# Order of the key blocks in the causal attention stage of a transformer block: diagonal blocks moved ahead of the plain ones

## Chip, cores and metric

The kernel runs on one core of a Trainium2 chip. The metric is the device time of one execution in microseconds (us). Before the change the median of three runs is 844.02 us (841.11 to 846.14).

## The reference

Input x is (2, 1024, 256), fp32. The block is an adaLN transformer layer:

```
h = layernorm(x) * (1 + ca) + sa
q, k, v = h@wq, h@wk, h@wv          # 32 query heads, 8 key/value heads, head size 8
att = softmax(causal(q k^T / sqrt(8)))
x = x + ga * ((att v) @ wo)
h = layernorm(x) * (1 + cb) + sb
x = x + gb * (shared MLP(h)/5 + top-4-of-16 experts(h) * 4/5)
```

The change touches only the causal softmax attention: for every query row the exponentials of the scores against all keys at or before it, and their products with v. A sum over key blocks may be taken in any order.

## The kernel before

**The attention stage.** Work is done in 16 groups (2 batches x 8 key/value heads, 4 query heads each). The queries of a group, 1024 rows, are two halves of 512; the keys are eight blocks of 128, c = 0 to 7. `half_steps` (L58) lists the steps of a half as (half, blocks, slots). Half 0 has three steps: block 0, then block 2, then blocks 1 and 3 side by side. Half 1 has seven: blocks 0, 1, 2, 3, 4, then block 6, then 5 and 7. Ten steps, numbered 0 to 9, make `STEPS`. A diagonal block (0, 1, 2, 3 of half 0, and 4, 5, 6, 7 of half 1) needs a causal mask; blocks 0 to 3 of half 1 are plain. Block c covers only the queries from its diagonal on, so block 6 (and 2) has 256 columns for each head and fits in one score slot instead of two.

**One step on TensorE (L1322 to L1339).** In this order: score slot 0 (`scores`, L1246), one `wide` product (L1182), score slot 1, one `narrow` product (L1194), then the product of the probabilities of the step two back with v (`product(s - 2)`, L1265), then the third slot if the step has one. Score slots take turns on two pairs of PSUM banks: slot k may be written once ScalarE is done with slot k - 2 (`released`, L1197). `wide` and `narrow` belong to a pass one and a half groups ahead that finds the row maxima; VectorE reduces them (L1434 to L1454), ten pairs per group. Pair number 5 + s of the next group runs in step s below 5, pair s - 5 of the group after it in the steps from 5 on.

**ScalarE (L1007 to L1044)** takes the slots in the same order: an exponential of 128x1024 (L1034), for the one-slot blocks L1029, and in the slots listed in `DIFF_AT` a Relu of 128x1024 (L960, `exceeding`). Such a slot holds a product of the queries with differences of keys (`differences`, L1221) for a later group: entry (s, slot): (which, ahead). Difference 0 and 1 are for the group two ahead, 2 for the next. The Relu result (`over`, `over6`) goes into the narrow reductions of tiles 6 and 7. Difference 0 waits for the late keys of that group (`ky_in`, loaded by SyncE, L666). The sums of the previous group are copied in step 1 (L1000), w_hi is filled in step 8 of groups 0 to 3 (L1044), and a square root with its table loads stands in step 3 of group 14.

**GpSimd (L852 to L898)**, in order by step: the mask of each diagonal step (`affine_select`, L862, waits for that step's exponentials); w_lo in step 4 of groups 1 to 4 (L869); in step 5 `split_rows` (L833, L835), which prepares the row maxima of the next group once VectorE has turned them; in step 6 one piece of other work: in groups 2 to 9 a 1.5 MB fill of a DRAM buffer with zeros (L879), later some small products. In step 8 of the last group one scatter (L540).

**SyncE (L719 to L741)**, in order for a group: when all score slots of the group before are full, the stacks and the late keys for the group two ahead (L475, L477, L488), the sums out (L708), then `rows_in`: four writes of the split row maxima to DRAM (L697, waits for `split_rows`), a wait for their landing, two loads of them into the query stack (L702), then the score keys for the group two ahead (L488). The next group's step 0 waits for those two loads (`row_in`, L1233).

After the attention stage come the output product, routing, the shared MLP and the expert tiles, behind a barrier of all engines.

```
L58  def half_steps(half):
L93  DIFF_AT = {(1, 1): (2, 1), (6, 2): (0, 2), (8, 1): (1, 2)}
L94  SLOT_ORDER = [(s, k) for s in range(NSTEP) for k in range(3 if (s, 2) in DIFF_AT else 2)]
L418 DIAG = [s for s, (half, blocks, _) in enumerate(STEPS) if blocks[0] >= half * (TC // 2)]
```

Of the kernel before, what the change touches and what calls it, by code (L numbers as in the profile page):

```python
# [56 lines left out]

def half_steps(half):  # L58
    d = half * (TC // 2)
    return [(half, (c,), 2) for c in range(d + 1)] + [(half, (d + 2,), 1), (half, (d + 1, d + 3), 2)]  # L60


STEPS = half_steps(0) + half_steps(1)
NSTEP = len(STEPS)
SCORE_SLOTS = sum(n for _, _, n in STEPS)
# [24 lines left out]


DIFFS = 3
DIFF_AT = {(1, 1): (2, 1), (6, 2): (0, 2), (8, 1): (1, 2)}  # L93
SLOT_ORDER = [(s, k) for s in range(NSTEP) for k in range(3 if (s, 2) in DIFF_AT else 2)]  # L94

DIFF_FREE = (0, 8 - NPAIR, 4)
# [23 lines left out]
def block_kernel(nc, x_in, wq_in, wk_in, wv_in, wo_in, wr_in, we1_in, we3_in, we2_in,  # L120
# [11 lines left out]
    with whole:  # L132
# [478 lines left out]
        def slots(group, s):  # L611

            return SCORE_SLOTS * group + sum(n for _, _, n in STEPS[:s + 1])

        def banks_of(group, s, slot):
            first = 2 * ((len(SLOT_ORDER) * group + SLOT_ORDER.index((s, slot))) % 2)
            return slice(first, first + 2)
# [7 lines left out]
        with nc.Block() as block:  # L625
# [277 lines left out]
            def _(act):  # L903
# [98 lines left out]
                def early_sums():  # L1002
                    act.wait_ge(pv_done, NSTEP * (GROUPS - 1) + len(half_steps(0)))
                    act.wait_ge(y_out, 16 * (GROUPS - 1))
                    act.activation(y_sb[:, 0, :], bank[sum_bank][:, :], ACT.Copy).then_inc(y_done, 1)

                for group in range(GROUPS):  # L1007
                    for s, (half, blocks, n) in enumerate(STEPS):
# [9 lines left out]
                        to = probs[(NSTEP * group + s) % (LAG + 1)]  # L1018
                        for slot in range(3 if (s, 2) in DIFF_AT else 2):
                            banks = banks_of(group, s, slot)  # L1020
                            if (s, slot) in DIFF_AT:
                                which, ahead = DIFF_AT[s, slot]
                                if group + ahead < GROUPS:
# [24 lines left out]
            def _(pe):  # L1048
# [148 lines left out]
                def released(group, s, slot):  # L1197
# [5 lines left out]
                    if group < 0:  # L1203
                        if before == -2:
                            pe.wait_ge(over_done, DIFFS + 2)
                    elif (s, slot) not in DIFF_AT:
                        pe.wait_ge(p_full, slots(group, s) - STEPS[s][2] + 1 + slot)
                    elif group + DIFF_AT[s, slot][1] < GROUPS:
                        which, ahead = DIFF_AT[s, slot]
# [42 lines left out]
                def product(group, s):  # L1252

                    half, blocks, n = STEPS[s]
                    if s == 0 and group:
                        pe.wait_ge(y_done, group)
                    elif group == GROUPS - 1 and s == len(half_steps(0)):
                        pe.wait_ge(y_done, GROUPS)
                    pe.wait_ge(p_full, slots(group, s))
                    if s in DIAG:  # L1260
                        pe.wait_ge(p_masked, NDIAG * group + DIAG.index(s) + 1)
                    for c, off, col, width in pieces(half, blocks):
                        at = HD + 1 + (group * TC + c) * VB - half * (HD + 1)
                        for h in range(REP):
                            last = pe.matmul(bank[sum_bank][32 * h:32 * h + 32, off:TT], v_aug[:, at:at + 32],  # L1265
                                             probs[(NSTEP * group + s) % (LAG + 1)][:, h, col:col + width], start=(s == 0),
                                             stop=(s == NSTEP - 1), skip_group_check=True)
                    last.then_inc(pv_done, 1)
# [711 lines left out]
```

## Time and profile before

| | |
|---|---|
| median of three runs | 844.02 us |
| the profiled execution | 843.63 us |
| its span | 841.4 us |
| TensorE busy | 722.4 us (86%) |
| VectorE busy | 540.6 us (64%) |
| ScalarE busy | 494.4 us (59%) |
| GpSimd busy | 269.8 us (32%) |
| mean granted TensorE clock | 0.92 |

The profile is of one execution. Its own time is 843.63 us, 2.2 us more than its span. PE is TensorE's matmuls and PEld its weight loads, DVE is VectorE, ACT ScalarE, POOL GpSimd, SP SyncE. The attention groups run from about 83 us to 480 us of the span. In a row of the timeline the columns are start, length, engine, line, operation, out<-in, shape, count, and in brackets how long the engine had been idle and what released it.

### The profile page before, as it was taken

Reading aid. Unit: us, or ns where it says so; the run is one execution under the profiler, and the core shown is the slowest. Engines: PE = TensorE matmul, PEld = TensorE weight load, DVE = VectorE, ACT = ScalarE, POOL = GpSimd, SP = SyncE. Lnnn points to the kernel's source line nnn. Section 1 sums busy time; section 2 is a strip of 40 time slices with the busy share of each in tenths; the row PEclk is TensorE's granted clock in tenths of the full one; section 3 lists DMA queues with packets and bytes.
Section 4 is the critical chain, followed back from the end, with each engine's and each line's share of the span. In section 5 each row is a group of like instructions: output and inputs, shape, how many; then the busy total and the mean of one; then the engine's idle time right before and its main releaser. Section 6 shows DMA issues by size and latency. Waiting matters only on the chain. (4 is left out here: it accounts for less than half of the span.)

```text
span 841.4 us, 14770 instructions
## 1 busy us (share of the span) xinstructions
PE 722.4 (86%) x4980; PEld 455.9 (54%) x4980; DVE 540.6 (64%) x1159; ACT 494.4 (59%) x739; POOL 269.8 (32%) x332
## 2 busy tenths in 40 slices
PE   8999999999999999999989881898149967999495
PEld 7466444444444444444435460786138846788384
DVE  7667888888888888888676431657025524665177
ACT  4332599998888898889566610574016624663132
POOL 6520133323222223323111466003730061412641
PEclk9989699999999999999988986899559978999898
DMA  6846234555545543354000287034325554653322
GB/s 208 209 123 169 82 90 102 145 165 152 146 144 154 158 146 104 92 137 136 17 14 17 70 278 242 7 114 157 125 97 162 163 163 132 205 178 116 98 69 81
DMA packets 78580, 108.71 MB, mean 129 GB/s; under 512 B 16200, under 2 KB 60040, under 8 KB 77420
## 3 DMA queue, kind: packets, MB, share of 16 engines
q1 hardware_dynamic: 67996, 77.16, 32.1%
q0 software_dynamic: 9280, 29.11, 10.5%
q10 hardware_dynamic: 1232, 1.51, 0.6%
q8 instruction: 42, 0.69, 0.4%
q14 instruction: 30, 0.25, 0.1%
HBM read 59.92 MB, written 47.39 MB: 128 GB/s over the span
## 5 line engine op out<-in xcount | busy, mean ns | idle before, releaser
L1034 ACT ACTIVATE probs<-psum 128x1024 f32<-128x1024 f32 x256 | 246.9, 1027 | 49.7 <-PE psum L1246 49.2
L1434 DVE TENSOR_REDUCE max_parts<-psum 128x2 f32<-128x1024 f32 (+2 forms) x160 | 196.0, 1225 | 68.8 <-PE psum L1182 66.9
L1265 PE MATMUL psum<-probs,v_aug 128*32 128x512 f32 (+3 forms) x1536 | 162.6, 512 | 0.3 <-POOL probs L862 0.2
L862 POOL TENSOR_SCALAR_AFFINE_SELECT probs<-probs 128x512 f32<-128x512 f32 (+1 forms) x96 | 79.2, 826 | 225.9 <-ACT probs L1034 206.3
L1246 PE MATMUL psum<-qs,ks 64*128 64x512 f32 (+3 forms) x768 | 138.3, 400 | 11.3 <-ACT over L960 5.0
L1246 PEld LDWEIGHTS psum<-qs,ks 64*128 64x128 f32 x768 | 67.2, 190 | 110.5 <-ACT probs L1034 69.4
L1769 PE MATMUL psum<-w_all,v_aug 128*128 x376 | 102.2, 396 | 0.9 <-issue 0.8
L1678 ACT ACTIVATE v_aug<-psum 128x128 f32<-128x128 f32 x94 | 26.1, 277 | 103.8 <-PE psum L1769 59.6
L1670 ACT ACTIVATE v_aug<-psum,modc 128x128 f32<-128x128 f32 x188 | 75.7, 454 | 12.5 <-remote 8.8
L1182 PE MATMUL psum<-km,qs 64*128 64x128 f32 (+2 forms) x608 | 76.3, 325 | 5.8 <-DVE max_parts L1434 2.7
L1769 PEld LDWEIGHTS psum<-w_all,v_aug 128*128 128x128 f32 x376 | 74.1, 199 | 13.1 <-issue 2.3
L1861 DVE TENSOR_TENSOR v_aug<-v_aug,psum 128x128 f32<-128x128 f32 x94 | 26.9, 287 | 76.2 <-ACT v_aug L1678 66.0
L1631 POOL DMA_INDIRECT h_t<-y_sorted,posi x32 | 31.0, 969 | 128.2 <-DMA y_sorted<-late 88.2
L1265 PEld LDWEIGHTS psum<-probs,v_aug 128*32 128x32 f32 x1536 | 34.4, 111 | 67.7 <-issue 62.9
L1194 PE MATMUL psum<-km,qs 64*128 64x512 f32 x160 | 66.5, 416 | 0.4 <-DVE max_parts L1453 0.2
L1780 PE MATMUL psum<-ident,v_aug 128*128 128x128 f32 x94 | 27.1, 288 | 46.3 <-issue 26.1
L1182 PEld LDWEIGHTS psum<-km,qs 64*128 64x128 f32 x608 | 52.0, 191 | 17.5 <-DVE max_parts L1434 9.8
L1786 PE MATMUL psum<-w_all,v_aug 128*128 x188 | 60.9, 408 | 0.0
L960 ACT ACTIVATE over<-psum 128x1024 f32<-128x1024 f32 x48 | 49.3, 1026 | 10.9 <-DVE max_parts L1453 5.1
L540 POOL DMA_INDIRECT x_sorted<-probs,posi x32 | 30.7, 960 | 66.3 <-DVE posi L309 56.9
L1874 DVE TENSOR_TENSOR late<-psum,gate 128x256 f32<-128x256 f32 x94 | 39.5, 420 | 19.2 <-remote 9.0
L1648 ACT ACTIVATE km<-wmod_sb 128x512 fp32r<-128x512 f32 x16 | 10.1, 631 | 62.5 <-remote 35.0
(194 smaller groups left out, 1076.2 us busy)
## 6 DMA issues: line engine op xcount, KB each, us to landing
late<-x_sorted SPq DMA_DIRECT2D x94, 128.0 KB
y_sorted<-late SPq DMA_DIRECT2D x94, 128.0 KB
x_sorted<-g_rows POOLq DMA_DIRECT2D x6, 1536.0 KB, 7.4
qs<-q_parts SPq DMA_DIRECT2D x62, 128.0 KB
km<-k_parts SPq DMA_DIRECT2D x62, 96.0 KB
km<-k_parts SPq DMA_DIRECT2D x64, 64.0 KB
ks<-k_parts SPq DMA_DIRECT2D x64, 64.0 KB
y_sums<-g_sign SPq DMA_DIRECT2D x16, 256.0 KB, 2.8
```

Source lines behind the costliest of these rows:

```text
L862: pool.affine_select(out=tile, in_=tile, compare_op=ALU.is_ge, fill=0.0, base=0, pattern=[[0, REP], [0, n], [1, P]], channel_multiplier=-1 ...
L960: act.activation(to, psum[:, banks, :], ACT.Relu).then_inc(over_done, 1)
L1034: act.activation(to[:, 2 * slot:2 * slot + 2, off:TT], psum[:, banks, off:TT], ACT.Exp, scale=SCALE).then_inc(p_full, 1)
L1182: last = pe.matmul(bank[wide_bank + hp][:, k * w:(k + 1) * w], qs[buf][rows, hh, i * P:(i + 1) * P], km[buf][rows, at:at + w], start=(k == ...
L1194: pe.matmul(bank[narrow_bank][:], qs[buf][rows, hh, i * P:(i + 1) * P], km[buf][rows, KU:KU + TT], start=True, stop=True).then_inc(narrow_ ...
L1246: last = pe.matmul(bank[first + hp][:, to:to + width], ks[buf][rows, c * P:(c + 1) * P], qs[buf][rows, hh, half * TT + off:(half + 1) * TT ...
L1265: last = pe.matmul(bank[sum_bank][32 * h:32 * h + 32, off:TT], v_aug[:, at:at + 32], probs[(NSTEP * group + s) % (LAG + 1)][:, h, col:col ...
L1434: dve.tensor_reduce(out=max_parts[:, :, h0:h1, slice(*tiles), slot], in_=psum[:, wide_bank:wide_bank + 2, :].rearrange("p a (s w) -> p (a ...
L1670: last = act.activation(xt[:, k % 2, c * P:(c + 1) * P], bank[X_BANKS[k % 2]][:, c * P:(c + 1) * P], ACT.Identity, scale=modc[:, b, 1, c, ...
L1769: last = pe.matmul(bank[U_BANKS[k % 2]][:, 0:2 * H], xt[:, k % 2, c * P:(c + 1) * P], w_all[:, bass.ds(expert[k], 1), c * 2 * H:(c + 1) * ...
L1786: pe.matmul(bank[Y_BANKS[k % 2]][:, 0:D], gt[:, k % 2, :], w_all[:, bass.ds(expert[k], 1), W13:WCOLS].rearrange("p a n -> p (a n)"), start ...
L1874: dve.tensor_tensor(out=yt[:, k % NY, :], in0=bank[Y_BANKS[k % 2]][:, 0:D], in1=gate[:, 1, k // TILES, :], op=ALU.mult).then_inc(y_copied, 1)
```

## The change

In half 1 the steps are now block 0, then block 4, then block 6, then blocks 5 and 7, then the plain blocks 1, 2, 3. So steps 4, 5, 6 are the diagonal ones and 7, 8, 9 the plain ones; before, steps 4, 5, 6 were plain (blocks 1, 2, 3) and 7, 8, 9 diagonal (4, 6, 5 and 7). Half 0 stays. Difference 0 moves from the third slot of step 6 to the free second slot of step 5, difference 1 from the second slot of step 8 to a third slot of step 7. Everything that is bound to a step's number (maxima pairs, split_rows, w_lo, the fill, w_hi) keeps its number. `DIAG` follows from the list.

```
 def half_steps(half):
     d = half * (TC // 2)
-    return [(half, (c,), 2) for c in range(d + 1)] + [(half, (d + 2,), 1), (half, (d + 1, d + 3), 2)]
+    return [(half, (0,), 2)] + [(half, (d,), 2)] * (half > 0) + [(half, (d + 2,), 1), (half, (d + 1, d + 3), 2)] + \
+        [(half, (c,), 2) for c in range(1, d)]
...
-DIFF_AT = {(1, 1): (2, 1), (6, 2): (0, 2), (8, 1): (1, 2)}
+DIFF_AT = {(1, 1): (2, 1), (5, 1): (0, 2), (7, 2): (1, 2)}
```

## Rows read from the trace of the kernel before

**Rows 1.** Busy time by stretch: one stretch of steady groups, one of group 13

```profile
180.00:240.00 60.00, 58.92 (x534) 27.94 (x530) 50.35 (x82) 54.30 (x59) 18.59 (x24) 1.00 0.51 141
...
426.00:429.00 3.00, 2.54 (x13) 1.04 (x17) 2.96 (x14) 1.86 (x2) 0.96 (x2) 0.61 0.00 0
```

**Rows 2.** Timeline, TensorE, from step 2 of one group to step 2 of the next

```profile
301.99 0.51 PE L1246 MATMUL psum<-qs,ks 64*128 64x384 f32 x4
...
304.44 0.50 PE L1246 MATMUL psum<-qs,ks 64*128 64x512 f32 x2
...
306.14 0.49 PE L1246 MATMUL psum<-qs,ks 64*128 64x512 f32 x2
...
307.03 0.51 PE L1246 MATMUL psum<-qs,ks 64*128 64x512 f32 x2
...
308.69 0.50 PE L1246 MATMUL psum<-qs,ks 64*128 64x512 f32 x2
...
311.02 0.50 PE L1246 MATMUL psum<-qs,ks 64*128 64x512 f32 x2
...
312.15 1.06 PE L1265 MATMUL psum<-probs,v_aug 128*32 128x512 f32 x8
...
313.61 0.50 PE L1246 MATMUL psum<-qs,ks 64*128 64x512 f32 x2
...
314.76 0.50 PE L1246 MATMUL psum<-qs,ks 64*128 64x512 f32 x2 [0.42 <-ACT over L960]
...
316.42 0.50 PE L1246 MATMUL psum<-qs,ks 64*128 64x256 f32 x4
...
320.77 0.50 PE L1246 MATMUL psum<-qs,ks 64*128 64x512 f32 x2
...
322.46 0.50 PE L1246 MATMUL psum<-qs,ks 64*128 64x256 f32 x4
...
323.37 0.49 PE L1221 MATMUL psum<-km,qs 64*128 64x512 f32 x2
...
325.02 0.51 PE L1246 MATMUL psum<-qs,ks 64*128 64x384 f32 x4
```

**Rows 3.** Timeline, ScalarE, same group

```profile
305.04 3.77 ACT L1034 ACTIVATE probs<-psum 128x1024 f32<-128x1024 f32 x4 [0.48 <-PE psum L1246]
...
313.68 1.03 ACT L960 ACTIVATE over<-psum 128x1024 f32<-128x1024 f32 x1
...
314.60 1.93 ACT L1034 ACTIVATE probs<-psum 128x1024 f32<-128x1024 f32 x2
```

**Rows 4.** Line L1044, all its instructions (ns min/median/max)

```profile
L1044 ACT ACTIVATE w_hi<-wmod_sb x4: 846/846/847, 111.4 to 180.6; 128x768 fp32r<-128x768 f32 x4
```

**Rows 5.** Timeline, TensorE, the last product of the attention stage

```profile
478.61 1.07 PE L1265 MATMUL psum<-probs,v_aug 128*32 128x384 f32 x16 [0.23 <-POOL probs L862]
```

**Rows 6.** Timeline, GpSimd and SyncE, same group as rows 2

```profile
302.24 4.11 SPq L488 DMA_DIRECT2D km<-k_parts  x6
...
309.60 0.21 POOL L833 CAST neg_parts<-neg_max_t 128x32 fp32r<-128x32 f32 x1 [3.88 <-DVE neg_max_t L1465]
...
310.18 1.73 SPq L697 DMA_DIRECT2D max_rows<-neg_parts  x4
...
316.89 0.55 SPq L702 DMA_DIRECT2D qs<-max_rows  x2
```

**Rows 7.** Line L862, all its instructions of one group (ns min/median/max)

```profile
L862 POOL TENSOR_SCALAR_AFFINE_SELECT probs<-probs x6: 677/678/1099, 298.1 to 318.1; 128x512 f32<-128x512 f32 x4, 128x1024 f32<-128x1024 f32 x2
```

**Rows 8.** Timeline, SyncE, group 10, which has no fill

```profile
333.57 1.75 SPq L697 DMA_DIRECT2D max_rows<-neg_parts  x4
337.05 0.53 SPq L702 DMA_DIRECT2D qs<-max_rows  x2
```

**Rows 9.** DMA issues: KB each, median us from issue to landing

```profile
x_sorted<-g_rows POOLq DMA_DIRECT2D x6, 1536.0 KB, 7.4
...
wmod_sb<-in_L_ffn_ws_dram SPq DMA_DIRECT2D x12, 128.0 KB, 2.6
```

## The prediction

> **What bounds it now.** I read the busy time by stretch first: in 60 us of steady groups TensorE is busy 58.92 us and ScalarE 54.30 [rows 1]. Two engines are nearly full, so the order in which they hand slots to each other can matter. Then the timeline of one group, step by step [rows 2]. A group takes 325.02 - 301.99 = 23.03 us. The first score products of steps 2 to 1 start at 301.99, 304.44, 306.14, 308.69, 311.02, 313.61, 316.42, (step 9 has no row) 320.77, 322.46.
>
> An undisturbed step is step 6 without its third slot: 1.13 us from its first score product to its v product (311.02 to 312.15), then 0.99 us to the next work; 2.12 us. The third slot adds 0.47 (313.61 - 311.02 - 2.12). A v product of a one-slot block is shorter: step 3, whose product is that of block 2, takes 1.70, so 0.42 less. Steps 2 and 5 take 2.45 and 2.33 for reasons that stay with their number or with half 0 (a maxima product in many pieces, about 0.2; blocks side by side, about 0.1). Three steps are longer than this: step 4, 2.55 for 2.12; step 7, 2.81 for 2.12; step 1, 2.56 for 2.12. The excess is 0.43, 0.69 and 0.44, together **1.56 us of stall** a group, and each lies ahead of the second slot: that starts 0.89, 1.15 and 0.91 us after the first (307.03, 314.76, 323.37), 0.46 without a stall.
>
> Who is late is seen on ScalarE [rows 3]. Back to back, ScalarE takes 0.94 to 0.97 us a slot, and TensorE may write slot k about 1.05 us after ScalarE began slot k - 2: the Relu begins at 313.68, the slot it frees starts at 314.76. ScalarE begins about 0.60 us after the score products start (304.44, 305.04). So where TensorE's steps are short (3 and 0, 1.70 us, against 1.94 for two slots) or ScalarE has three slots (step 6, and step 1 with the copy of the sums), the next second slot comes late. One slot of buffering takes up the rest.
>
> **The change, part by part.**
>
> *Order of the steps.* The light v product (block 6) leaves step 0 and goes to step 7, two after its block. Step 0 becomes 2.12 us for ScalarE's 1.94, so ScalarE no longer enters step 1 late: the 0.44 of step 1 goes. Step 3 is still 1.70, so the 0.43 of step 4 stays.
>
> *Third slot.* It moves from step 6 to 7, where it meets that light product: TensorE needs 2.12 - 0.42 + 0.47 = 2.17 us, ScalarE three slots, 2.9. Followed with the numbers above, from the first score product of step 7 at 0: exponentials begin at 0.60 and 1.57, the Relu at 2.54, step 8's first slot may start at 1.57 + 1.05 = 2.62 (0.45 late), its second at 2.54 + 1.05 = 3.59 at the earliest, where 2.62 + 0.47 = 3.09 would be free: 0.50 late. So 0.95 in place of step 7's 0.69. Step 0 gets about 0.03. Sum of stalls after: 0.43 + 0.95 + 0.03 = 1.41 for 1.56: **0.15 us less a group**, 13 steady groups (0 to 12), -1.9 us. The same recurrence put on the order before gives 0.45, 0.65 and 0.45, so it is good to 0.1 a group, 1.3 us in all.
>
> *w_hi* [rows 4], 0.85 us of ScalarE, groups 0 to 3. It followed step 8 when ScalarE had a gap; now it follows the run of slots that bounds step 8. Bounds: nothing, or 0.85 x 4 = 3.4 us. Step 9 has 0.15 to 0.2 of slack a step and the stall of step 0 is gone, so I take 0.2 a group, +0.8.
>
> *Groups 13 and 14*, where output products and transposes make TensorE wait for VectorE; the work of TensorE is the same. The clock is already down to 0.61 in a stretch of group 13 [rows 1]. A light product moved beside waits: between -0.5 and +0.5, zero taken. Slots without a difference product make small bubbles in groups 14 and 15; before there were as many.
>
> *Masks.* The last v product of the stage waited 0.23 for GpSimd [rows 5]; now it needs no mask, but the product ahead of it is full, 0.42 more: +0.2. Otherwise the masks of steps 4 to 6 (0.68 us, 1.10 for blocks side by side) [rows 7] have over a step before the v product wants them, and no TensorE row of the group waits for GpSimd. The scatter that stood ahead of the last masks loses its place there; the scatters start sooner, but what follows waits for the barrier.
>
> *GpSimd's queue.* `split_rows` now stands behind the masks of steps 4 and 5. It began at 309.60 [rows 6], 0.91 after step 5 (308.69). The exponential of step 5's one slot ends at 0.60 + 1.03 = 1.63 after it (a slot of the same size in [rows 3]), the mask takes 0.68, so it begins at 2.3: 1.4 us later. The fill is issued behind the mask of step 6: its second exponential ends 1.57 + 1.03 = 2.6 us after step 6's start, the mask takes 1.1; step 6 starts 2.33 after step 5, so the fill leaves at 6.1 after step 5, where it was right behind `split_rows`. SyncE's chain: the four writes of the maxima start at 2.9 (before 1.49). With the fill beside them, SyncE had to wait from 311.91 to 316.89 for their landing; without it (group 10) from 335.32 to 337.05, 1.7 us [rows 6, 8]. Now they are out before the fill: 2.9 + 1.75 + 1.7 = 6.4 after step 5, where it was 8.2. SyncE comes to its loads sooner. The next step 0 comes 12.1 after step 5, so the loads have 5.7 us; they now run beside the fill. I take that as hidden, cost 0.
>
> *Difference 0* is wanted at step 5's second slot, near 309.4, and no longer behind step 6's v product (312.15 + 0.99 = 313.14). Its keys are the last four of the loads issued up to 302.24 + 4.11 = 306.35 [rows 6]; a load of 128 KB lands 2.6 us after issue [rows 9], and the last one is issued at 305.7, so by 308.3. Margin 1.1 us, cost 0.
>
> Sum: -1.9 + 0.8 + 0 + 0.2 = -0.9 us on the profiled 843.63, that is 842.7. The median of the runs is 0.4 above that execution: **843.1**. A measurement of this kernel tells about 0.5% (4.2 us) from no change, so this is no difference.
>
> **Rivals.**
>
> *A, faster.* The stall of step 1 goes and the one of step 8 does not grow. For it: the recurrence takes ScalarE's 0.97 a slot, and runs of four go at 0.94; 0.44 x 13 = 5.7 less. Against it: three slots in a row cannot be had under 2.8 us. Time 843.6 - 5.7 = 837.9, say 838.
>
> *B, slower: the row maxima meet the fill.* Place: the two loads L702, waited for at the next step 0. They leave at 6.4 after step 5 and the fill at 6.1. The writes in the same position before waited until 316.89, while the fill, issued right behind `split_rows` (309.60 and half a microsecond) and 7.4 us from issue to landing [rows 6, 9], ended near 317.5. If the loads too land only with the fill, that is 6.1 + 7.4 = 13.5 after step 5, where step 0 wants them at 12.1: 1.4 us in each of 8 groups, 11 us, 855. It decides from 5.7 us of landing on; the writes needed 5.0 to 6.7. Against it: the fill's data starts later than its issue, and the loads have a head start.
> The Trainium skill (DMA: Bandwidth & Descriptors, Queues, rings and completion order) says that each DMA engine takes turns between its queues a packet at a time. By that rule, the loads share rather than wait, and the trace agrees so far: the writes [rows 6] were stretched and not stopped.
>
> *C, slower: late keys.* If their landing takes 4.2 us from issue, difference 0 waits 0.5 us in 12 groups, 6 us: 849. Against it: the 2.6 us of a larger load.
>
> *D, slower: the clock.* Step 8 now has two stalls in a row, 0.95. In group 13, after waits of 0.4 to 0.75, the clock fell to 0.61 for 3 us [rows 1]. One such fall a group, 1.5 us each, 13 groups: 20 us, 863. Against it: 0.69 in one step left it at 1.00.
>
> **Numbers.** Forecast 0.68, A 0.12, B 0.11, C 0.05, D 0.04. Of the forecast's case 0.03 lies under -4.2 us. Faster 0.15, same 0.65, slower 0.20. The range reaches down to A and up to C with w_hi's upper bound (3.4 in place of 0.8), 838 to 852, which leaves out B's price, D and a little of A, under 0.2.
>
> **What would show it.** Right: group period 22.8 to 23.0; step 1 without a stall; step 8 near 3.1 us; step 7 at 2.17; writes L697 about 1.4 us later after step 5, and the wait ahead of L702 under 2 us in all groups. Wrong: a wait for `qs<-max_rows` or `km<-k_parts` ahead of step 0 or step 5, a clock under 1.00 before group 13, step 0 longer than 2.5 in groups 1 to 4, or a period off by more than 0.3.

## Result and profile after

The changed kernel takes 850.32 us, median of 19 runs, beside 844.58 us for the kernel before, also in 19 runs: ratio 1.0059, 95% interval [1.0031, 1.0087]. The medians are of all runs; the ratio, here and below, leaves out runs in a slower state, more than 1.5% above the fastest of their kernel. It is 5.0 us slower by the ratio, a little more than the 0.5% that counts as a difference. The forecast was 843.1 us, 0.9 less than before, and "same"; the time lies within the stated range of 838 to 852, but it moved the other way. The profiled execution took 851.17 us.

First the page of after, span and busy times:

```profile
span 849.4 us, 14770 instructions
PE 718.0 (85%) x4980; PEld 452.8 (53%) x4980; DVE 542.5 (64%) x1159; ACT 493.7 (58%) x739; POOL 268.8 (32%) x332
```

The engines do nearly the same work (TensorE 718.0 us busy, 722.4 before; ScalarE 493.7 and 494.4); what changed is mostly waiting. Line numbers are one higher than before. Next the timeline of TensorE over one group of after, the answer to [rows 2], from step 2 (302.97) to the next step 2 (325.79):

```profile
302.97 0.50 PE L1247 MATMUL psum<-qs,ks 64*128 64x384 f32 x4
...
305.41 0.49 PE L1247 MATMUL psum<-qs,ks 64*128 64x512 f32 x2
...
307.11 0.50 PE L1247 MATMUL psum<-qs,ks 64*128 64x512 f32 x2
...
309.67 0.50 PE L1247 MATMUL psum<-qs,ks 64*128 64x256 f32 x4
...
312.00 0.50 PE L1247 MATMUL psum<-qs,ks 64*128 64x384 f32 x4
...
314.24 0.50 PE L1247 MATMUL psum<-qs,ks 64*128 64x512 f32 x2
...
315.94 0.50 PE L1222 MATMUL psum<-km,qs 64*128 64x256 f32 x4
...
316.83 0.50 PE L1247 MATMUL psum<-qs,ks 64*128 64x512 f32 x2 [0.39 <-ACT probs L1035]
...
317.75 0.50 PE L1247 MATMUL psum<-qs,ks 64*128 64x512 f32 x2 [0.18 <-ACT over L961]
...
319.41 0.49 PE L1247 MATMUL psum<-qs,ks 64*128 64x512 f32 x2
...
321.53 0.51 PE L1247 MATMUL psum<-qs,ks 64*128 64x512 f32 x2
...
323.67 0.50 PE L1247 MATMUL psum<-qs,ks 64*128 64x256 f32 x4
...
325.79 0.50 PE L1247 MATMUL psum<-qs,ks 64*128 64x384 f32 x4
```

This group takes 22.82 us, 23.03 before. Step 1 is 2.12 (323.67 to 325.79): its stall is gone. Step 4 keeps its own (2.56). Step 8's first slot comes 2.59 after step 7's, 0.42 more than the 2.17 of work, and its second 0.92 after the first, 0.46 late. That is the hand recurrence of the prediction almost to the row (0.45 and 0.50 late).

But not every group is such a group. From one copy of the sums (L1001) to the next, the twelve steady periods after the first copy are 22.93, 22.96, 23.86, 23.60, 23.12, 22.82, 23.28, 22.82, 22.83, 23.65, 22.82 and 22.81 us; before all lay between 23.02 and 23.09. Their sum is 277.5, 276.6 before, and would be 273.8 at 22.82 throughout. One of the long ones, SyncE and TensorE of after (group 4; group n is the period from its own copy in step 1 to the next group's):

```profile
188.01 3.42 SPq L489 DMA_DIRECT2D km<-k_parts  x5
...
195.51 0.49 PE L1222 MATMUL psum<-km,qs 64*128 64x512 f32 x2 [0.61 <-DMA km<-k_parts]
```

The product L1222, difference 0, waits for the late keys. Without a wait it now comes 7.13 us after the copy of the sums (11.0 before), and the issue of the last load ends only at 191.43; the product runs 4.1 us later. In group 3 (23.86) the same product comes 8.03 us after the copy, after 0.75 us of idle time that the trace puts down to ScalarE. Since the same slot needs no wait in other groups, the keys are the likely cause there too; the trace doesn't name them.

The same stretch as [rows 6], GpSimd and SyncE of after:

```profile
312.00 0.21 POOL L834 CAST neg_parts<-neg_max_t 128x32 fp32r<-128x32 f32 x1
...
312.57 1.73 SPq L698 DMA_DIRECT2D max_rows<-neg_parts  x4
315.36 0.55 SPq L703 DMA_DIRECT2D qs<-max_rows  x2
315.96 4.15 SPq L489 DMA_DIRECT2D ks<-k_parts  x4
...
315.66 1.08 POOL L880 DMA_DIRECT2D x_sorted<-g_rows  x1
```

The maxima are written 2.9 us after step 5 (309.67), as said, and are reloaded 1.06 us after the end of that issue; before, the fill stretched it to 5 us. What the fill stretches instead is the issue of the score keys behind it, 4.15 us here, 2.74 in groups without a fill. SyncE comes to the next loads later than it could.

Second, the end of the stage. GpSimd, TensorE, VectorE and ScalarE of after:

```profile
472.68 1.10 POOL L541 DMA_INDIRECT x_sorted<-xn,posi  x1 [2.30 <-DVE posi L310]
...
479.19 0.96 POOL L541 DMA_INDIRECT x_sorted<-xn,posi  x1 [0.30 <-issue]
...
477.06 1.07 PE L1266 MATMUL psum<-probs,v_aug 128*32 128x512 f32 x8
478.06 1.16 PE L580 MATMUL psum<-k_parts_sb 128*128 128x128 f32 x8
482.12 5.38 PE L569 MATMUL psum<-c_rep,v_aug 128*128 128x256 f32 x16 [2.90 <-DVE v_aug L551]
...
481.29 0.69 DVE L551 TENSOR_TENSOR v_aug<-v_aug,psum 128x512 f32<-128x512 f32 x1 [3.36 <-remote]
...
479.10 0.60 ACT L1001 ACTIVATE g_sign<-psum 128x512 f32<-128x512 f32 x1 [3.62 <-issue]
490.82 1.28 ACT L1655 ACT_TABLE_LOAD   x1 [11.12 <-PEq L626]
```

In the brackets, `remote` is a release by something that the profile doesn't know, `issue` idle time for which it shows no wait. And the same place in the unchanged kernel before (run c_before, below):

```profile
477.68 1.07 PE L1265 MATMUL psum<-probs,v_aug 128*32 128x384 f32 x16 [0.23 <-POOL probs L862]
478.68 1.16 PE L579 MATMUL psum<-k_parts_sb 128*128 128x128 f32 x8
480.71 3.69 PE L568 MATMUL psum<-c_rep,v_aug 128*128 128x256 f32 x16 [0.87 <-DVE v_aug L550]
...
479.88 0.69 DVE L550 TENSOR_TENSOR v_aug<-v_aug,psum 128x512 f32<-128x512 f32 x1 [1.63 <-PE psum L579]
...
478.98 0.60 ACT L1000 ACTIVATE g_sign<-psum 128x512 f32<-128x512 f32 x1 [2.61 <-PE psum L1265]
487.81 1.28 ACT L1654 ACT_TABLE_LOAD   x1 [8.23 <-PEq L625]
```

From the last v product to ScalarE's first work behind the barrier: 13.8 us after (477.06 to 490.82), 10.1 before (487.81 - 477.68). VectorE begins its second product (L551) 3.2 us after TensorE's spread (478.06) instead of 1.2; VectorE's input was complete at 479.22 (end of L580); it starts 1.14 us after the end of the last scatter (480.15). TensorE stands for 2.90 us, and its next product takes 5.38 us instead of 3.69 at a lower clock: the granted clock is 0.69 from 482.0 to 487.5, while the same product of c_before ran at 1.00. In the new order six scatters of GpSimd follow each other without a break, because no mask of the last steps stands between them.

The two profiled executions are 8.0 us of span apart. By landmarks: +0.1 up to the first copy of the sums, +0.9 in the twelve periods, -1.6 in group 13, -1.3 in group 14, +1.1 in the last group, +2.9 from its copy to the barrier, together +2.1; then +5.9 behind the barrier (358.6 against 352.7). The last part is not read as an effect: two more profiles of the old order have 355.4 and 358.4 there.

### The profile page after: what moved, and what is told of

The parts are those of the page before. It is cut to its first block and busy times, and to the rows that moved or that the text cites. A ratio compares the mean times of both kernels' runs of the same rounds, so it can differ in the third digit from the quotient of the medians.

```text
span 849.4 us, 14770 instructions
## 1 busy us (share of the span) xinstructions
PE 718.0 (85%) x4980; PEld 452.8 (53%) x4980; DVE 542.5 (64%) x1159; ACT 493.7 (58%) x739; POOL 268.8 (32%) x332
## 5 line engine op out<-in xcount | busy, mean ns | idle before, releaser
L1266 PE MATMUL psum<-probs,v_aug 128*32 128x512 f32 (+3 forms) x1536 | 159.6, 504 | 0.0
L1247 PE MATMUL psum<-qs,ks 64*128 64x512 f32 (+3 forms) x768 | 136.0, 394 | 13.4 <-ACT probs L1035 8.9
L1247 PEld LDWEIGHTS psum<-qs,ks 64*128 64x128 f32 x768 | 65.3, 186 | 121.8 <-ACT probs L1035 65.5
L1770 PE MATMUL psum<-w_all,v_aug 128*128 x376 | 101.7, 395 | 0.9 <-issue 0.8
L1770 PEld LDWEIGHTS psum<-w_all,v_aug 128*128 128x128 f32 x376 | 74.1, 199 | 13.0 <-issue 2.3
L1266 PEld LDWEIGHTS psum<-probs,v_aug 128*32 128x32 f32 x1536 | 34.0, 109 | 66.6 <-issue 61.2
L1183 PEld LDWEIGHTS psum<-km,qs 64*128 64x128 f32 x608 | 49.2, 188 | 17.8 <-DVE max_parts L1435 10.1
L541 POOL DMA_INDIRECT x_sorted<-probs,posi x32 | 30.8, 962 | 66.2 <-DVE posi L310 56.8
L1649 ACT ACTIVATE km<-wmod_sb 128x512 fp32r<-128x512 f32 x16 | 10.1, 631 | 69.8 <-remote 42.9
```

Source lines behind the costliest of these rows:

```text
L1183: last = pe.matmul(bank[wide_bank + hp][:, k * w:(k + 1) * w], qs[buf][rows, hh, i * P:(i + 1) * P], km[buf][rows, at:at + w], start=(k == ...
L1247: last = pe.matmul(bank[first + hp][:, to:to + width], ks[buf][rows, c * P:(c + 1) * P], qs[buf][rows, hh, half * TT + off:(half + 1) * TT ...
L1770: last = pe.matmul(bank[U_BANKS[k % 2]][:, 0:2 * H], xt[:, k % 2, c * P:(c + 1) * P], w_all[:, bass.ds(expert[k], 1), c * 2 * H:(c + 1) * ...
```

## Experiments

Each run is timed beside the kernel before, on its own chip, and every ratio is to that. They came on four chips of two kinds: on the one of c_before to e6 and the one of f1 to f4, as in the result, the kernel before takes 844 to 849 us; on the one of e0 to e3 and the one of g1 to g4 it takes 746 us. "Steady sum" is the twelve periods, "stretch" the last v product to the barrier, both of the one profiled execution. In the expectations, theory K is that late keys took the gain, S that the six scatters in a row slow the end of the stage, V that only the executions vary.

**e0, the changed kernel again (746 us chip).** No edit.

> The changed kernel once more, for a second trace of it. Theory S (the end of the attention stage): the group period is 22.8 us where no key load is late, 23.7 where one is; the last stretch, from the last v product (L1266) to the start behind the barrier (L1655), is again about 13.8 us, against 10.1 in the trace before. Theory V (the executions only vary behind the barrier): that stretch comes out at 10 to 11 us this time. Ratio to before 1.003 to 1.009 by both.

Measured: 748.54 us, 1.0022 [0.9994, 1.005]. Steady sum 277.9, with waits for `km<-k_parts` in four groups (0.20 to 0.51 us). Stretch 10.03. So the late keys are there on this chip too, the long stretch is not; the interval includes no difference.

**e1, no scatter in the stage.**

```
-        AMONG = {8: (0,)}
-        SCATTERED = 6
+        AMONG = {}
+        SCATTERED = 0
```

> The changed kernel with all scatters of the first batch behind the barrier (AMONG empty, SCATTERED 0). Theory S: six scatters that now run in a row during the last steps slow the end of the stage (VectorE's second L551 came 3.2 us after its product began instead of 1.2, and TensorE's clock fell); without them the stretch from the last v product to the barrier is 10 to 11 us and the time falls by 3 to 4 us, to a ratio near 1.001. Rival V: the stretch stays as it is or varies, ratio 1.005 or more, since the scatters behind the barrier also start 7 us later.

Measured: 758.5 us, 1.0166 [1.0136, 1.0196]; stretch 10.03 as in e0, the first expert tile 8.3 us later. The expected gain did not come, since there was no long stretch here to shorten. On this chip, moving all six out costs far more (some 10 us against e0) than they could cost where they are.

**e2, scatters 1 to 5 held until the last slots.**

```
+                pool.wait_ge(p_full, slots(GROUPS - 1, NSTEP - 1))
                 for k in range(1, SCATTERED):
```

> The changed kernel, scatters 1 to 5 held until the last exponentials are done, as the masks of steps 8 and 9 held them before the change; scatter 0 stays in step 8. Theory S: stretch from last v product to barrier 10 to 11 us, ratio near 1.001. Rival V: no difference to the changed kernel, 1.005.

Measured: 748.81 us, 1.0039 [1.0022, 1.0057]; stretch 10.03. No gain on this chip, where there was nothing to repair. Its steady sum is 279.8: group 4 took 25.53, with 2.50 us of wait for `qs<-max_rows` at 206.10. That is rival B, in one group.

**e3, row maxima split ahead of step 5's mask.**

```
+                        if s == 5 and group + 1 < GROUPS:
+                            split_rows(group + 1)
                         if s in DIAG:
...
-                        if s == 5 and group + 1 < GROUPS:
-                            split_rows(group + 1)
```

> The changed kernel with split_rows put ahead of the mask of step 5 in GpSimd's queue (the fill stays in step 6). Theory K (late keys): SyncE's writes of the maxima start 1.4 us earlier, its loads of the score keys are issued before the fill's data flows, the key loads of the next group are not late, so the waits of difference 0 for km<-k_parts are gone and all steady groups take 22.8 us: 3 to 4 us less than the changed kernel, ratio near 1.001. Rival: the score key loads are still issued beside the fill (it starts 0.1 to 1 us after them), waits stay in the groups that had them, ratio 1.005.

Measured: 747.27 us, 1.0008 [0.9989, 1.0027]; steady sum 279.0, with four waits for `km<-k_parts` (up to 1.34) and none for `qs<-max_rows`. The waits did not go, as the rival had it: an earlier split alone does not bring the keys in time.

**c_before, the kernel before again (849 us chip).**

> The kernel of before, unchanged, for its trace on the chip of these runs. Both theories: group period 23.03 to 23.06 in all steady groups, no wait for km<-k_parts, ratio 1.00. It gives the stretches behind the steady groups (group 13, 14, 15, last v product to barrier, barrier to end) against which the changed kernel's are read.

Measured: 845.94 us, 1.0003 [0.9965, 1.004]; steady sum 276.6, stretch 10.13.

**e4, late keys loaded earlier:** SyncE takes the late keys of group + 3 behind the row maxima, instead of those of group + 2 ahead of them, and the score keys ahead of the maxima.

```
-                        late_keys(group + 2)
...
-                    if group + 1 < GROUPS:
-                        rows_in(group + 1)
                     if 1 <= group < GROUPS - 2:
                         score_keys(group + 2)
+                    if group + 1 < GROUPS:
+                        rows_in(group + 1)
+                    if group < GROUPS - 3:
...
+                        late_keys(group + 3)
```

> The changed kernel with SyncE's queue reordered: score keys right behind the sums, late keys of the group three ahead behind the maxima rows, so that they land some 10 us before difference 0 wants them. Theory K (late keys are what gives back the gain): no wait for km<-k_parts, all steady groups but the tenth at 22.8 us, the twelve periods together 274.7 against 277.9 in the changed kernel and 276.6 before; 3 us less than the changed kernel, ratio 0.995 to 0.998. Rival (DMA queue): the stacks are then late instead, since the transfers are the same; periods stay at 23.1 on average, ratio 1.002.

Measured: 854.41 us, 1.0067 [1.0017, 1.0117]. Difference 0 waits for keys in no group (0.33 us is left once, ahead of a `wide` product, L1188, in group 3), but group 4 takes 27.93 us, with 2.50 us of wait for `qs<-max_rows` and a lower clock behind it, and the stretch is 15.2 us. The steady sum is 280.7 where 274.7 was expected: the repair of one fault was hidden under two others.

**e5, the same edit on the kernel before.**

> The kernel of before with the same reordering of SyncE's queue. Theory K: nothing waited for these keys before, so the period stays 23.03 and the ratio 1.000. Rival (the reordering helps by itself, by spreading the transfers): ratio 0.998 or less.

Measured: 847.15 us, 0.9992 [0.9946, 1.0039]; steady sum 276.7, stretch 10.07. In the old order the edit neither helps nor hurts: the old order waits for no keys.

**e6, the new order with the differences a step later,** so that difference 0 has its old distance to the loads.

```
-DIFF_AT = {(1, 1): (2, 1), (5, 1): (0, 2), (7, 2): (1, 2)}
+DIFF_AT = {(1, 1): (2, 1), (5, 1): (0, GROUPS), (6, 2): (0, 2), (8, 2): (1, 2)}
```

> The changed order of steps, but difference 0 back in a third slot of step 6, difference 1 in a third slot of step 8, and the second slot of step 5 left empty. Theory K: difference 0 is wanted 4 us later, so no wait for km<-k_parts remains. The recurrence of the prediction gives a period of 23.7 us for this packing (two steps of three slots, an empty one before), so 12 x 23.7 = 284.6, and a ratio near 1.011. Rival (the slots do not matter, only the keys): period 22.9, ratio 0.997.

Measured: 856.25 us, 1.0116 [1.0058, 1.0174]. No wait for keys in any group; the period is 23.67 to 23.71 in the late groups, which is what the recurrence gave for this packing (step 5 with an empty slot, steps 6 and 8 with three); the steady sum is 286.9, 284.6 expected, and the stretch 14.9.

**f1, the changed kernel again (848 us chip).**

> The changed kernel unchanged, beside its variants. Theory S (six scatters issued back to back hold up the handoffs between engines until the last of them is through): from the last v product to the first activation behind the barrier 13 to 15.5 us on a chip where the tile stage begins near 552 us of the profile, 10.0 to 10.2 on one where it begins near 526. Theory V (the stretch of 13.8 was chance): 10 to 11 on either. The sum of the twelve steady periods 277 to 279 us, as late keys cost 3 to 4.5 of the 273.9 that undisturbed groups would take. Ratio 1.002 to 1.009.

Measured: 853.12 us, 1.0071 [1.0018, 1.0123]; steady sum 278.6 with five waits for `km<-k_parts` (0.34 to 1.31 us); stretch 13.95. ScalarE, VectorE and TensorE:

```profile
481.65 0.60 ACT L1001 ACTIVATE g_sign<-psum 128x512 f32<-128x512 f32 x1 [5.93 <-remote]
...
481.75 0.69 DVE L551 TENSOR_TENSOR v_aug<-v_aug,psum 128x512 f32<-128x512 f32 x1 [2.25 <-remote]
...
482.58 5.38 PE L569 MATMUL psum<-c_rep,v_aug 128*128 128x256 f32 x16 [3.11 <-DVE v_aug L551]
```

Both engines start within 0.1 us of each other, though TensorE had given them their input at 478.4 and 479.5 (ends of L1266 and L580): something held both, and let them go 1.25 and 1.35 us after the last scatter ended (480.40). The same start of VectorE comes 1.14 us (after) to 1.35 us (f1, e4) after the last scatter's end in all four long stretches; ScalarE is held that long in three of them, in after it starts at 479.10.

**f2, scatters held as in e2, on the same chip as f1.**

> GpSimd waits for the last step's probability slots before scatters 1 to 5, which gives them the place that they have in the kernel before. Theory S in its narrow form (what hurts is that scatters 0 to 5 stand in one row ahead of the end): scatter 0 stands apart, as before, and the stretch from the last v product to the barrier is 10 to 11 us instead of 13.8, the ratio 3 us lower than that of the changed kernel beside it (about 1.002). Rival, the row of five alone is enough in the new order, since two of the last steps' handoffs now fall beside it: the stretch stays 13 to 15 us. Theory V: no difference to the changed kernel beside it.

Measured: 850.59 us, 1.0054 [1.0024, 1.0083]; stretch 10.10:

```profile
479.30 0.60 ACT L1002 ACTIVATE g_sign<-psum 128x512 f32<-128x512 f32 x1 [2.72 <-issue]
...
480.41 0.69 DVE L551 TENSOR_TENSOR v_aug<-v_aug,psum 128x512 f32<-128x512 f32 x1 [1.39 <-PE psum L580]
...
481.25 3.69 PE L569 MATMUL psum<-c_rep,v_aug 128*128 128x256 f32 x16 [0.93 <-DVE v_aug L551]
```

The narrow form of theory S holds: five in a row (476.86 to 482.91 in this profile), with the first 2 us ahead of them, run beside the handoffs and leave them alone, as in the kernel before. The steady sum was 279.7, since the row maxima were late in group 4 again (2.50 us); the ratio alone could not have shown the repair, and its interval and f1's overlap.

**f3, only scatters 0 to 2 in the stage** (`SCATTERED = 3`).

> Only scatters 0 to 2 of the first image are issued in the attention stage, 3 to 5 go behind the barrier with the others. Theory S: two scatters in a row behind scatter 0 are too few to hold anything up, the stretch is 10 to 10.3 us on either kind of chip; behind the barrier GpSimd has three scatters more, up to 3.9 us, so the tile stage begins at most 3.9 us later than it does after the barrier now (by 0 to 3.9). Ratio 1.000 to 1.009. Theory V: the stretch is as in the changed kernel beside it, and the three scatters cost up to 3.9 us more.

Measured: 850.65 us, 1.0063 [1.0026, 1.0101]; stretch 10.03, steady sum 282.0 (five waits for keys, up to 1.67 us). The first expert tile begins 67.8 us behind the barrier, 65.1 in f1 and 63.1 to 66.2 in the other profiles of the slower chips. The stretch is mended; part of it is probably paid behind the barrier. The third scatter ends at 479.29, ahead of the handoffs (481.14), so this run says what happens without scatters beside them, not how many in a row do harm.

**f4, all three repairs:** the edits of e2, e3 and e4 together.

> All three repairs on the new order: SyncE loads the late keys of group+3 behind the row maxima instead of group+2 ahead of them, the row maxima are split ahead of step 5's mask, and scatters 1 to 5 wait for the last slots. Theory K (late keys took the gain) with S: no wait for km, nor for the row maxima in group 4 (their write 0.7 to 1.1 us earlier, ahead of the fill), so all periods at 22.8 to 22.95 except group 10's 23.65: sum 274.5 to 276; the stretch to the barrier 10 to 11. Against the kernel before -1.5 in the steady groups, -1.6 and -1 to -2 in groups 13 and 14: ratio 0.993 to 0.998 (-2 to -5 us). If the stretch stays long: 0.998 to 1.003. If the row write meets the fill all the same in one group (2.5 us of wait and a lower clock behind it, 5 us as with the early keys alone): 5 us more than that.

Measured: 843.41 us, 0.9924 [0.9887, 0.9961]. Steady sum 275.5, stretch 10.10, one wait for keys (0.26, a `wide` product in group 3), none for the maxima. This version beats both kernels: by the ratios 6.4 us faster than before, 12.5 faster than the changed kernel beside it.

**g1 to g4, one repair withdrawn at a time (746 us chip).** First g1, f4 again.

> The kernel with the three repairs again, beside the same kernel with one of them withdrawn. Steady sum 274 to 276 us, stretch from the last v product to the barrier 10.0 to 10.2, ratio 0.989 to 0.997 on a chip where the tile stage begins near 552 us, 0.993 to 0.998 where it begins near 526. If its first result was chance, 0.998 to 1.003.

Measured: 742.78 us, 0.9957 [0.9936, 0.9978]; steady sum 275.0, stretch 10.03. No wait for keys or maxima.

g2 is g1 without the wait ahead of the scatters.

> Repaired kernel without the wait ahead of scatters 1 to 5, so that all six follow each other. Theory S: the stretch to the barrier is 13.5 to 15.5 us instead of 10.1 and the last group 23 instead of 19.9, while the first activation behind the barrier comes 3 to 7 us later; ratio 0.004 to 0.007 above that of the repaired kernel beside it. On a chip like the one where the tile stage began near 526 us: no difference. Steady sum unchanged, 274 to 276.

Measured: 741.9 us, 0.9948 [0.9928, 0.9968]; steady sum 275.8, stretch 10.03. No difference on this chip, as in e2. On a slower chip this repair was not withdrawn from the three.

g3 is g1 with the late keys in their old place.

> Repaired kernel with the late keys back in their place ahead of the sums and the row maxima. Theory K: waits of difference 0 for km of 0.3 to 1.3 us in 3 to 6 of the groups 3 to 13 and, with the row maxima that now leave earlier, the fill beside other transfers; steady sum 277.5 to 280 instead of 275.5; ratio 0.003 to 0.006 above the repaired kernel's. Rival, the split ahead of the mask alone repairs it: steady sum 275 to 276, ratio equal.

Measured: 746.58 us, 1.0007 [0.9989, 1.0025]; steady sum 277.3, with waits of 1.19 and 0.58 us for `km<-k_parts`.

g4 is g1 with the row maxima split behind step 5's mask.

> Repaired kernel with the row maxima split behind step 5's mask again, as in the changed kernel. If the 5.1 us of group 4 with the early keys alone come from the order of the row maxima and the fill: their write is issued at 10.2 us of groups 1 to 4 instead of 9.6 and in one of the groups 1 to 4 the maxima land late, with 2 to 3 us of wait for qs and a lower clock behind it; steady sum 279 to 281, ratio 0.004 to 0.007 above the repaired kernel's. If that was a rare meeting: steady sum 274.5 to 276, ratio within 0.002 of the repaired kernel's.

Measured: 745.62 us, 1.0007 [0.9988, 1.0027]; steady sum 279.7, of it group 4 26.93. GpSimd, SyncE and TensorE of g4:

```profile
194.95 1.82 POOL L875 TENSOR_TENSOR w_lo<-wmod_sb,w_hi 128x768 fp32r<-128x768 f32 x1
196.73 0.67 POOL L868 TENSOR_SCALAR_AFFINE_SELECT probs<-probs 128x512 f32<-128x512 f32 x1
197.37 0.20 POOL L839 CAST neg_parts<-neg_max_t 128x32 fp32r<-128x32 f32 x1
...
200.11 1.04 POOL L885 DMA_DIRECT2D x_sorted<-g_rows  x1
...
197.94 1.73 SPq L698 DMA_DIRECT2D max_rows<-neg_parts  x4
202.30 1.33 SPq L703 DMA_DIRECT2D qs<-max_rows  x2
...
208.53 0.69 PE L1253 MATMUL psum<-qs,ks 64*128 64x512 f32 x2 [2.48 <-DMA qs<-max_rows]
```

and of g1:

```profile
196.75 1.73 SPq L698 DMA_DIRECT2D max_rows<-neg_parts  x4
199.53 0.53 SPq L703 DMA_DIRECT2D qs<-max_rows  x2
...
199.57 1.04 POOL L885 DMA_DIRECT2D x_sorted<-g_rows  x1
```

In groups 1 to 4, w_lo (1.82 us) stands ahead of the mask and of `split_rows`. In g4 the loads go out 2.2 us behind the fill's issue and 6.2 us ahead of the product that waits for them; in g1 they go out just before it, and nothing waits. The windows 208.00:213.00 of g4 (first) and of f2 (second), right behind the same wait of 2.5 us; the columns are TensorE, weight loads, VectorE, ScalarE and GpSimd busy, then granted clock, DMA share and GB/s:

```profile
208.00:213.00 5.00, 4.47 (x23) 2.06 (x24) 1.89 (x3) 2.11 (x3) 0.67 (x1) 0.66 0.67 161
```

```profile
208.00:213.00 5.00, 4.95 (x44) 2.48 (x44) 3.78 (x6) 4.17 (x5) 1.35 (x2) 1.00 0.60 139
```

g4's execution loses the clock (0.66), f2's keeps it (1.00): the same wait costs 4.1 us of period or 2.5.

## Why the prediction was wrong

**Order of the steps and third slot: right.** 22.82 us a group against 23.05 on average (276.6 / 12), so 0.22 to 0.23 less (0.15 said, good to 0.1); steps 1, 4, 7 and 8 as worked out. That would be -2.7 us over twelve periods. The signs named for a right forecast are there in such a group (step 1 without a stall, the writes at 2.90 after step 5); the sign of being wrong that came is the wait for `km<-k_parts`, and in other executions the one for `qs<-max_rows`.

**w_hi: right in sign, somewhat too large.** The periods that hold it are 22.93 and 22.96 where it alone disturbs, 0.12 above 22.82; 0.2 was taken.

**Difference 0, "Margin 1.1 us, cost 0": the step that failed first.** It rested on one group's chain of loads and on the landing time of another load (2.6 us, [rows 9], counted from the last issue's start, which put the landing 2.0 us behind that issue's end). Before, the last of these loads is issued by 3.1 to 6.4 us after the copy of the sums, depending on the group; I had looked at a group with 4.2. And a waiting product runs as much as 4.1 us behind the end of the issue in after and 4.4 in e3, not 2.0. Wanted at 7.13, keys whose issue ends at 3.7 or later are at times late. All nine profiled executions that have the new order, difference 0 in step 5 and the late keys in their old place show waits for `km<-k_parts`, in two to five of the twelve groups each; the old order and e6 show none ahead of this product. g3 against g1 prices it: 2.2 us of steady sum in one profile each, 3.8 us in the medians (intervals [0.9989, 1.0025] and [0.9936, 0.9978]). It was rival C, at a chance of 0.05, with less than the 0.5 us in every group that it assumed.

**GpSimd's queue, "the loads have 5.7 us; I take that as hidden, cost 0": right for most groups, wrong for group 4.** The sum for `split_rows` left out w_lo, which stands ahead of it in groups 1 to 4 and makes it 0.9 us later still (10.2 us after the copy instead of 9.3). Rival B then happens in group 4 alone, in five of ten executions whose split stays behind the mask (0.86 us once, 2.5 four times), and in none of five with the split ahead of it. g4 against g1: 4.7 us of steady sum in one profile each, 2.8 in the medians (g4's interval [0.9988, 1.0027]). That the loads share with the fill rather than wait for it is how the text read the Trainium skill's rule (DMA: Bandwidth & Descriptors, Queues, rings and completion order). The trace agrees that they get through beside it, but not that sharing is cheap: 6.2 us from the issue in g4.

**Masks, "the scatters start sooner, but what follows waits for the barrier": the third failed step.** What follows does wait for the barrier, but the work that leads to the barrier shares the end of the stage with the scatters. Without the masks between them, all six run in a row, and on the slower kind of chip the stretch grew from 10.1 us to between 13.8 and 15.2 in all four profiles of the new order that leave the scatters as they are, with a granted clock of 0.50 to 0.69 during the product L569 that follows the wait, 1.00 in c_before and f2; holding the scatters (f2, f4) or cutting them to three (f3) brings back 10.0 to 10.1 in three of three. On the two faster chips it is 10.03 in all eight profiles, so there the sentence holds. The forecast had no rival for this. What in the row of six holds the other engines, its length without a break or its place ahead of the handoffs, no run parts: six in a row as late as in f2 were not tried. Nor is the stretch priced in run times: f1 and f2 differ by 0.0017 in the ratio, within their intervals.

**Groups 13 and 14, zero taken.** Group 14 takes 27.9 to 29.0 us in the new order on the slower chips (26.7 in f3) and 30.2 to 30.3 in the old: a gain of 1.2 us or more. In group 13 the two orders touch (33.9 to 34.5 against 34.4 to 35.6). I have not traced the cause.

**The sum.** For the profile up to the barrier: -2.7 for the order (twelve periods of 22.82 instead of 276.6 us), +3.6 given back in the periods (some 2.5 in groups 3, 4, 5 and 7, where the key product comes late, 0.8 by a stall of group 10, below, the rest w_hi), -2.9 in groups 13 and 14, +4.0 for the end of the stage, +0.1 at the start, which makes the +2.1 above. Of the 5.0 us that the ratio gives (2.6 to 7.3 by its interval) this leaves some 3 behind the barrier or in stalls that differ by execution (steady sums of the changed kernel and near variants run from 277.5 to 282.0). New-order profiles of the slower chips have 352.2 to 361.3 us behind the barrier (seven, mean 358.2), old-order ones 352.7 to 358.4 (three, mean 355.5). That may be chance; whether the order has any effect there stays open.

Group 10's 23.65 stays in the repaired kernels too, 0.8 above its neighbours (0.2 in e6). It has no wait for keys in g1. Its trace shows VectorE with 1.74 us of other work there (`g_sign`, L1510, at 9.2 us after the copy), a `wide` product (L1189) idle for 0.65 us on VectorE behind it, and a score slot 0.62 us on ScalarE behind that. Before, the same work cost TensorE 0.27 us of idle time and the period nothing (23.06). So it is another margin that the new order spent; no run tests it.

## What to carry to other kernels

Moving a consumer earlier spends slack that one group's rows do not show: take the latest producer over all groups, and everything that stands ahead of it on its queue in any of them (here w_lo in four). When work that looked like cover is taken from between a burst of indirect DMA issues, read what the other engines do beside that burst. And when a change moves several margins at once, repair them together and then withdraw one at a time: the ratio of each repair alone (e2, e3, e4, f2, f3) is within 0.002 of an unrepaired kernel's on the same kind of chip, all three gave 0.9924 on a slower chip and 0.9957 on a faster one.

## What the chips showed that was not expected

Six indirect scatters in a row (7.5 us of GpSimd) went with a hold of ScalarE and VectorE in f1 until 1.25 us after the last one; the long stretch was there on both slower chips and on neither of the two faster. The same division shows behind the barrier, where 26 scatters follow each other. The windows 488.00:525.00 of after (slower chip) and 485.00:519.00 of e0 (faster one), with TensorE, weight loads, VectorE, ScalarE and GpSimd busy, then clock, DMA share and GB/s:

```profile
488.00:525.00 37.00, 17.79 (x78) 14.72 (x76) 9.77 (x25) 3.11 (x4) 25.01 (x26) 0.76 0.79 263
```

```profile
485.00:519.00 34.00, 28.80 (x160) 25.32 (x161) 19.66 (x43) 14.91 (x21) 25.67 (x26) 0.90 0.84 282
```

The scatters take about the same time, but on the slower chip TensorE gets 78 records in instead of 160. The first expert tile begins at 553.9 there and at 525.8 here, and the tile stage, from its first product with `w_all` (L1770) to the last, takes 214 us against 155. The attention stage is equal on both (22.82 us in an undisturbed group), and the spans behind the barrier are 358.6 and 256.3 us, so the 100 us between the chips lie behind the barrier. That indirect DMAs are what makes them is not shown, and why the chips differ, no run here shows. A verdict on such a kernel should name the chip; the ratios of the changed kernel, 1.0071 [1.0018, 1.0123] on one and 1.0022 [0.9994, 1.005] on the other, do not differ beyond their intervals.
